# Reordering the first 50 microseconds of a fused attention and expert kernel: which work goes ahead of the first score step

## The reference

```python
def reference(x, w_attn, w_proj, decay_raw, W1, W2, Wr):      # x: 8 x 512 x 128
    xn = layernorm(x)                       # over the 128 channels
    # attention, 16 heads of 8 channels, causal
    q, k, v = split(xn @ w_attn)
    logw = -log1p(softplus(decay_raw)[h] * log1p(distance))
    y = softmax(q @ k.T / sqrt(8) + causal + logw) @ v
    attn = y @ w_proj
    # experts: 8 of them, the best 2 for each token
    probs = softmax(xn @ Wr.T); gate = top 2 of probs, normalised
    ffn = sum over the 2 experts of gate * (silu(xn @ W1[e].T) @ W2[e].T)
    return x + attn + ffn
```

## Time and profile before

| | us |
|---|---|
| median of 3 runs | 505.39 (504.28 to 505.66) |
| the profiled execution | 506.12 |
| its span, first to last instruction | 504.4 |
| what lies around the span | 1.72 |
| mean granted TensorE clock | 0.997 |
| PE busy over the span | 478.1 (95%) |
| DVE, POOL, ACT busy | 365.7, 366.2, 336.6 |

### The profile page before, as it was taken

The page is one execution under the profiler, slowest core; times in us unless marked ns, Lnnn a source line. Parts: engine busy times, 40 slices in busy tenths (PEclk is TensorE's granted clock), DMA queues, the critical chain, the costliest instruction groups (busy, mean ns, idle before and its releaser), DMA issues.

```text
span 504.4 us, 13425 instructions
## 1 busy us (share of the span) xinstructions
PE 478.1 (95%) x4294; PEld 346.7 (69%) x4294; DVE 365.7 (73%) x1407; ACT 336.6 (67%) x621; POOL 366.2 (73%) x591
## 2 busy tenths in 40 slices
PE   6769899999999999999999999989999999999997
PEld 5645465555664665566566556689999999999564
DVE  7888989988999989989889897733333333333887
ACT  4789878888888888887988888752233233232762
POOL 3587987889888889889889888734454554555784
PEclk9998999999999999999999999999999999999999
DMA  6479790780470461353255153877676777672634
GB/s 188 126 278 286 201 215 16 213 199 18 133 215 28 143 182 57 122 158 102 90 159 138 51 183 112 227 223 238 199 210 208 210 208 207 191 216 69 246 118 140
DMA packets 72755, 82.24 MB, mean 163 GB/s; under 512 B 8638, under 2 KB 52704, under 8 KB 72688
## 3 DMA queue, kind: packets, MB, share of 16 engines
q1 hardware_dynamic: 68368, 72.91, 50.3%
q0 software_dynamic: 4320, 8.47, 4.7%
HBM read 49.94 MB, written 31.86 MB: 162 GB/s over the span
## 4 chain that ended last, share of the span: by engine, by line
PE 69%; DVE 17%; ACT 10%; issue 2%; DMA 1%; SPq 0%; ACTq 0%; DVEq 0%
PE psT L1498 22%; PE psT L1585 13%; PE ps L1558 12%; PE psO L1518 11%; DVE scores L1268 8%; PE ps L1470 6%; ACT probs L1008 4%; ACT scores L965 3%; PE psM L1446 2%; DVE x_all L608 2%; PE ps L1549 1%; ACT values L992 1%; DVE xt L1122 1%; DMA w_qkv<-w_attn 1%; DVE probs L1054 1%
## 5 line engine op out<-in xcount | busy, mean ns | idle before, releaser
L1268 DVE CUSTOM_DVE_ANT_0 scores<-ps,wdist 128x256 f32<-128x256 f32 (+3 forms) x512 | 217.3, 485 | 22.6 <-PE ps L1470 21.8
L1008 ACT ACTIVATE probs<-psT 128x512 f32<-128x512 f32 x320 | 173.8, 597 | 50.3 <-PE psT L1498 49.1
L875 POOL TENSOR_SCALAR scores<-scores,row_max 128x256 f32<-128x256 f32 (+3 forms) x388 | 185.3, 493 | 29.2 <-DVE row_max L1268 28.1
L1498 PE MATMUL psT<-ident,scores 128*128 128x128 f32 x1280 | 176.3, 281 | 5.7 <-ACT probs L1008 5.6
L1498 PEld LDWEIGHTS psT<-ident,scores 128*128 128x128 f32 x1280 | 137.7, 141 | 64.0 <-issue 46.3
L894 POOL DMA_INDIRECT picked_dram<-scores,row_ring x71 | 69.8, 983 | 70.0 <-DVE scores L1349 66.8
L1017 ACT ACTIVATE scores<-ps 128x512 f32<-128x512 f32 x71 | 42.3, 598 | 91.4 <-PE ps L1558 91.4
L1518 PE MATMUL psO<-probs,values 128*32 128x512 f32 (+3 forms) x1024 | 88.4, 441 | 0.0
L965 ACT ACTIVATE scores<-scores,row_max 128x512 f32<-128x512 f32 x124 | 83.0, 727 | 0.0
L1585 PE MATMUL psT<-xn_all,scores 128*128 x568 | 75.4, 276 | 1.6 <-ACT scores L1017 1.6
L1558 PE MATMUL ps<-scores,wdist 128*128 128x128 f32 x568 | 74.9, 275 | 0.6 <-DMA wdist<-w1t 0.6
(11 more groups left out here) (169 smaller groups left out, 295.3 us busy)
## 6 DMA issues: line engine op xcount, KB each, us to landing
wdist<-w1t SPq DMA_DIRECT2D x71, 256.0 KB, 3.4
k_rows<-k_dram SPq DMA_DIRECT2D x64, 96.0 KB, 3.0
q_rows<-q_dram SPq DMA_DIRECT2D x64, 96.0 KB, 2.9
row_ring<-rows_dram SPq DMA_DIRECT2D x71, 65.0 KB, 2.9
rows_dram<-row_ring SPq DMA_DIRECT2D x6, 650.0 KB, 6.3
k_dram<-k_parts SPq DMA_DIRECT2D x7, 384.0 KB, 2.4
q_dram<-q_parts SPq DMA_DIRECT2D x7, 384.0 KB, 2.6
xn_all<-picked_dram SPq DMA_DIRECT2D x4, 512.0 KB, 7.4
```

Source lines behind the costliest of these rows:

```text
L875: last = nc.gpsimd.tensor_scalar(part, part, -1.0, row_max[:, r, tile, quad:quad + 1], ALU.mult, ALU.add)
L1008: nc.scalar.activation(probs[:, at.ring(2), w, :], psT[:, w % 2], ACT.Exp, scale=-1.0).then_inc(exp_ready, 1)
L1268: last = nc.vector.tensor_tensor_reduce(out=scores[:, r, u, col:col + n], in0=bank[:, col:col + n], in1=wdist[:, at.g * QUADS + quad, SEQ ...
L1498: last = nc.tensor.transpose(psT[:, w % 2, place * P:(place + 1) * P], scores[:, at.ring(2), u, col + key * P:col + (key + 1) * P], ident[:])
```

## The change

It alters the order of steps and the waits that go with it. No arithmetic is added or removed except warm-up matmuls.

1. The weights' DMA is issued ahead of the decay vector's.
2. `scaled_weights` leaves part 0 of BN and becomes a step of its own, WQ, behind NX. KA of batch 0 gets a wait for the centred weights.
3. The second warm-up stretch shrinks from 8 to 2.
4. In the prologue, BN part 1 is cut after 8 of its 12 tiles, and the last 4 with its sums and RS 1 go behind VL of batch 0. RT 0 goes from behind VL of batch 1 to behind VL of batch 3 and waits for that copy.
5. The turn of batch 6, VL of batch 4, and the turn of batch 7 (with LN 7) go ahead of the first score step; VL of batches 5, 6, 7 and LN 8 to 15 move up by one P1 step each in slot 0.
6. The last 4 tiles' statistics with the sums and RS of part 3 go into slot 1 (behind P1 steps 0 and 1). RT 1, RO 1 and LC go behind P1 step 4 of slot 1, CZ 2 behind step 3.
7. In slot 29, MI goes ahead of ACT's share of the maxima (SA). In slot 32, the second part of PV goes behind a TE step.

```diff
+EARLY = {0: {1: (("VL", 20), ("LN", 8), ("LN", 9)),
+             2: (("VL", 24), ("LN", 10), ("LN", 11), ("CZ", 1)),
+             3: (("VL", 28),) + tuple(("LN", h) for h in range(12, 16)) + (("TL", 0),),
+             4: (("XN", 4),) + ...
-         1: {2: tuple(("LC", b * GROUPS) for b in range(1, BATCH)) + (("CZ", 2),), 4: (("CZ", 3),)}}
+         1: {0: (("BN", 0, 3, 28, 32),), 1: (("RS", 3),), 3: (("CZ", 2),),
+             4: (("RT", 1), ("RO", 1)) + tuple(("LC", b * GROUPS) for b in range(1, BATCH)) + (("CZ", 3),)}}
...
-    step("PV", n - 2, NGROUP, 1)
+    if n != NGROUP:
+        step("PV", n - 2, NGROUP, 1)
...
+    if n == NGROUP:
+        step("PV", n - 2, NGROUP, 1)
     step("TE", n - 1, NGROUP, 4, 6)
...
+    if n == EXPERT_SLOT - 1:
+        steps.append(("MI", 0))
     if n >= GROUPS_BY_POOL:
         step("SA", n, NGROUP, (6, 7))
...
 PROLOGUE = [
-    ("BN", 0, 0, 0, 4), ("RS", 0), ("WU", 5), ("WC", 0), ("WU", 8), ("NX", 0), ("LN", 0), ("LN", 1), ("XB", 0), ("LN", 2),
-    ("KA", 0), ("QA", 0), ("BN", 0, 1, 4, 16), ("RS", 1), ("XB", 4),
+    ("BN", 0, 0, 0, 4), ("RS", 0), ("WU", 5), ("WC", 0), ("WU", 2), ("NX", 0), ("WQ", 0), ("LN", 0), ("LN", 1), ("XB", 0),
+    ("LN", 2), ("KA", 0), ("QA", 0), ("BN", 0, 1, 4, 12), ("XB", 4),
     ("KR", 0), ("QR", 0), ("KM", 0), ("QM", 0), ("KL", 0), ("QL", 0), ("LN", 3), ("CZ", 0),
     ("KW", 0, 0), ("QW", 0, 0), ("KD", 0), ("QD", 0),
-    ("XB", 8), ("VL", 0), ("BN", 0, 2, 16, 20), ("XB", 12), ("VL", 4), ("RT", 0), ("BN", 0, 2, 20, 24), ("RS", 2), ("LN", 4),
-    ("XB", 16), ("VL", 8), ("BN", 0, 3, 24, 32), ("RS", 3), ("LN", 5), ("XB", 20), ("VL", 12), ("LN", 6),
+    ("XB", 8), ("VL", 0), ("BN", 0, 1, 12, 16), ("RS", 1), ("XB", 12), ("VL", 4), ("BN", 0, 2, 16, 20), ("LN", 4),
+    ("XB", 16), ("VL", 8), ("BN", 0, 2, 20, 24), ("RS", 2), ("LN", 5), ("XB", 20), ("VL", 12), ("RT", 0), ("LN", 6),
+    ("BN", 0, 3, 24, 28), ("XB", 24), ("VL", 16), ("LN", 7), ("XB", 28),
     ("RO", 0), ("KW", 0, 1), ("QW", 0, 1), ("RB", 4), ("KD", 1), ("QD", 1), ("VS", 4), ("VS", 8), ("VS", 12)]
...
                 sp.dma_start(x_all[:, 0:TILES, :], x_rows(0)).then_inc(first_x_loaded, 16)
+                sp.dma_start(w_qkv[:], w_attn).then_inc(w_loaded, 16)
                 sp.dma_start(decay_in[:], decay_raw.rearrange("(a h) -> a h", a=1).broadcast_to([P, HEADS])
                              ).then_inc(decay_loaded, 16)
-                sp.dma_start(w_qkv[:], w_attn).then_inc(w_loaded, 16)
...
-                        scaled_weights()
                         dve.wait_ge(dve_init, 1)
...
-                run_prologue({**number_parts, "BN": norm_stats, "NX": normalise})
+                run_prologue({**number_parts, "BN": norm_stats, "WQ": scaled_weights, "NX": normalise})
...
-                    pe.wait_ge(vo_free, BATCH if n else 2)
+                    pe.wait_ge(vo_free, BATCH if n else 4)
...
-                    if b == 3:
+                    if b == 4:
                         pe.wait_ge(rstd_copied, 1)
-                    if b == 4:
                         pe.wait_ge(misc_free, MISC["KA", 0] + 1)
...
                         elif kind == "KA":
                             pe.wait_ge(xt_copied, 1)
+                            pe.wait_ge(centred_copied, 1)
```

More of the change, by code:

```diff
@@ L85 @@
 TOPK = 2
[L86 to L89, removed]
+EARLY = {0: {1: (("VL", 20), ("LN", 8), ("LN", 9)),
+             2: (("VL", 24), ("LN", 10), ("LN", 11), ("CZ", 1)),
+             3: (("VL", 28),) + tuple(("LN", h) for h in range(12, 16)) + (("TL", 0),),
+             4: (("XN", 4),) + tuple(
                  (kind, b * GROUPS) for kind, b in (("VS", 4), ("VS", 5), ("VS", 6), ("VS", 7), ("XS", 2), ("XS", 3), ("XS", 4),
                                                     ("XS", 5), ("XS", 6), ("XS", 7)))},
-         1: {2: tuple(("LC", b * GROUPS) for b in range(1, BATCH)) + (("CZ", 2),), 4: (("CZ", 3),)}}
+         1: {0: (("BN", 0, 3, 28, 32),), 1: (("RS", 3),), 3: (("CZ", 2),),
+             4: (("RT", 1), ("RO", 1)) + tuple(("LC", b * GROUPS) for b in range(1, BATCH)) + (("CZ", 3),)}}
 FIRST_ROWS_SLOT, ROW_TILES = 1, 4
@@ L246, in slot_steps @@
     steps.extend(("PA", 0, *part) for part in SUMS.get(n, ()))
-    if n == EXPERT_SLOT - 1:
-        steps.append(("MI", 0))
     if (n - 2) % PAIR == PAIR - 1:
@@ L1072, in norm_stats, with scaled_weights @@
                                                op0=ALU.max, op1=ALU.add).then_inc(decay_ready, 1)
-                def scaled_weights():
+                def scaled_weights(at):
                     dve.wait_ge(centred_full, 1)
```

## The result

The changed kernel takes 508.88 us (median of 10, 504.15 to 510.74) against 505.60 of before (median of 10, 503.04 to 506.87), a ratio of 1.0062 (95% interval 1.0033 to 1.0092): slower by 3.3 us, where 503.4 was forecast. The profiled execution took 504.15 us; the forecast of it was 504.07. It was the fastest of the ten and the only one with a granted clock of 1.000; the others had 0.986 to 0.993.

The account below looks back on a forecast made before the run. PE was taken to bound the middle (busy 95% of the span), so gains come only where it waits. Head start 1.65 plus 0.4 at R1 gave 2.05 us: 506.12 to 504.07, or 503.4 at the median; range 502.4 to 506.0.

Parts of the forecast that it names:

- Decay vector: Front, normalisation's chain: issued behind the weights, the vector delays it by 0.4 us, at worst 1.3.
- Clock: Front, PE: a low clock costs 0.2 us on the turn, half its price, and nothing on key and query products.
- the slower rival: Front: low clock lasts past the products through the next turns and first value product; 507.1 us, chance 0.11.
- Decay late: Front, rival: the decay vector lands with the weights, 0.9 us more on the normalisation; 504.3 us, chance 0.09.
- low clock: Front, two rivals: low clock through key and query products, 505.3 us, chance 0.20; or beyond them, 507.1, chance 0.11.
- nearest row: Phrase absent from the prediction given; on the clock it cites warm-up durations and 0.50 after a 2.40 us wait.
- 1.65: Front: the head start in us, 1.85 won at the turn less 0.2 for the clock.
- the 0.4 at R1: Slot 1, routing's first step R1: 0.4 us gained beyond the front's head start, bounds -0.5 and 1.6.
- WQ behind NX ... the new wait in KA is free: Front: two DVE copies cost 0.6 us, hidden by ACT's copy of the turned tokens; 0.3 without that cover.
- Slot 29 and the drain ... 0: Moving MI gains 0 us (bounds -0.3 and 0.2); moving a PV part in the drain 0 (to 0.1).
- Whatever this moment gains goes on to the end: From R1 on: the gain there persists, since what follows is work in fixed order with no fixed time.
- The scale: Whole kernel: the profiled run lies 0.73 us above the median 505.39, so 504.07 becomes 503.4 on the median's scale.

Follow-up runs that it names:

- e1: The changed kernel, unedited, run again: 511.18 us, ratio 1.0109; its profiled execution took 509.81 us.
- e17: The changed kernel with 12 more TensorE passes in slot 1, where it waits for the first exponentials: 508.34 us, ratio 1.0033.
- e3: The kernel before with only its second warm-up stretch cut from 8 to 2: 509.45 us, ratio 1.0060.
- e4: The kernel before with items 1 to 3 only (DMA order, WQ behind NX, 2 pairs of warm-ups): 509.05 us, ratio 1.0070.
- e15: The changed kernel, unedited, profiled once more: that execution took 507.54 us.
- e8: The kernel before with item 2 alone (WQ behind NX, and KA's wait): 505.61 us, ratio 0.9991.
- e6: The kernel before with items 4 to 7 alone: 505.95 us, ratio 1.0005.
- e5: The changed kernel with 8 pairs of warm-ups and the decay vector's DMA issued first again: 505.72 us, ratio 1.0002.
- e13: The changed kernel with six more pairs of warm-ups behind the turn of batch 0, ahead of the key product: 507.49 us, ratio 1.0024.
- e7: The changed kernel with 8 pairs of warm-ups, decay vector first, and 2 more pairs behind the first turn: 505.25 us, ratio 0.9985.

## Why the prediction was wrong, step by step

- **Decay vector: "I take 0.4 ... at worst it lands with the weights at 5.9 and costs 1.3 us".** This is the step that failed first, a term of the sum that was too small. In the eight profiles that have it behind the weights dec_neg came at 4.7, 5.3, 5.3, 5.5, 5.6, 5.8, 6.3 and 6.7: 0.1 to 2.1 later than the 4.60 of before, a median near 1. I had let one row, 2.8 us for a transfer that stood in front, speak for one that stands behind 196 KB. The bound was wrong too, in its reason: issued first, the weights land 2.8 to 3.0 us after 1.30, so at 4.1 to 4.3, not at 5.9 (nor only half a us earlier than before's 6.13), and in e1 the vector came 2.5 us after them, at 6.7. So "it lands with the weights" gives neither the time nor a bound. (The rule cited for it, "DMA: Bandwidth & Descriptors", Queues, rings and completion order, in the Trainium skill, agrees with the order in all eight: none came before the weights. It gives no price.) What it shares the engines with in those 2.5 us, the other tokens' DMA issued at 2.31 among it, wasn't tried.
- **Clock: "0.2 for the turn ... and nothing for the products".** This is the second step that failed, a term put at nothing. I had looked at the gap with a decay slip of 0.4, some 0.6 us. At 0.51 and 1.18 us it is indeed nothing (1.12 and 1.13 us for the key passes). At 1.43 to 3.11 it is 0.2 to 0.95 for the key passes, 0.7 to 0.9 for the query passes, and up to 0.9 for the next eight turns. The price per product (0.87) was about right (0.95 and 0.89 in e1). The point from which the slower rival decides, a low clock at VL of batch 0, was reached in e17 alone (1.56 us for its first eight passes); in e1, e3, e4 and e15 they took 1.09, as in after. It was named by the clock, not by what comes before it: PE's gap, that is the decay vector.
- **The rivals were kept apart.** "Decay late" stood at 504.3 with 0.09 and "low clock" at 505.3 and 507.1 with 0.20 and 0.11. They are one case: the late vector makes the gap that costs the clock, and item 3 took away the passes that would have covered it. The sum priced the 12 warm-ups at nothing but time. Together they give R1 at 46.5 to 48.5 and 507.5 to 509.8 us, outside the range. The slower rival had the right sign, 507.1, 1.8 us too little, and part of the mechanism: the low level does reach the next turns (1.55 us for eight in e1), but in no profile of the changed kernel the value product it counted in, and the late vector and the longer expert stretch, which do cost time, are not in it.
- **"nearest row" for the gap.** The before kernel has no gap there at all, so no row of it could show what a pause does ahead of the products. The row with a clock of 0.50 after the 2.40 us wait did show it elsewhere; I cited it and did not use it.
- **Where the vector was in time, the sum held, in part by luck.** XB 0 at 8.28 (8.75 forecast), first score step 22.02 (22.3), table load 31.06 (31.4), R1 43.81 (44.05) with DVE waiting 1.24 (1.6) for POOL's logits, the releaser I had named; own time 504.15 (504.07). Part of that is errors that cancel: the turn won 2.3 and not 1.65, and the 0.4 at R1 was not there (from turn to R1 35.5 us before and after; POOL ends last there where DVE did, at the same moment). The stretch of the experts took 0.6 more.
- **"WQ behind NX ... the new wait in KA is free"**: right (e8). **Items 4 to 7**: I gave them 0.4 at R1; e6 and e5 against e8 say 0. **"Slot 29 and the drain ... 0"**: no run told them from 0; they are in e6.
- **"Whatever this moment gains goes on to the end".** Half right: from R1 to the first expert turn it took 281.8 us before and 281.5 to 281.7 in the four profiles of after. The expert stretch, though, scatters by up to 3.6 us and was longer in nearly every profile with 2 pairs. That what follows is in a fixed order does not make its time fixed.
- **The scale.** I moved the sum from the profiled run to the median as if a kernel's executions lay as close as those three (504.28 to 505.66). The changed kernel's lie over 6.6 us, and in its four profiles it is the landing of one 8 KB transfer that goes with the clock its products get.

## What to carry to other kernels

Warm-ups that compute nothing cover a variable landing as well as hold the clock. Before shortening them, ask how late the last input of the next real matmul can be, not how late it was in one profile, and leave passes for that, but not without measure: 5 to 12 pairs took the same time here, 20 pairs 0.7% more. When an edit makes one engine wait for a transfer and another takes away what filled the wait, price the pair. If a profile agrees with a sum, compare its own time and its granted clock with the other runs before trusting it: here 504.15 us at 1.000 stood against a median of 508.88 at 0.991.

## What the runs showed of the hardware that I had not expected

- An 8 KB transfer issued behind one of 196 KB landed 2.8, 3.5, 3.5, 3.7, 3.7, 3.9, 4.4 and 4.9 us after its issue in eight profiles, and 2.7 to 3.3 in the twelve that have it first. The weights, in turn, landed 3.4 to 4.3 us after their issue as the second and 2.8 to 3.0 as the first.
- A pause of 1.18 us ahead of the turn left the key passes at 1.13 us and the query passes at 1.02. Key and query passes took 1.35 and 1.91 us behind a pause of 1.43, 2.07 and 1.71 behind 1.49 (e3), 1.36 and 1.91 behind 1.62, 2.08 and 1.91 behind 2.34 and 3.11. In e3 the four warm-ups ahead of the pause were at the high level already, in e4 and e15 (1.43 and 1.62) still at the low one. The length of the pause alone does not order the key passes.
- The clock that the profile prints does not show the low level at the start. From 6 to 8 it is 1.00 in the profile of after, where the four warm-ups take 421 ns each, and from 10 to 12 in e13, where ten passes do; at the high level such a pass takes 275. Durations tell the level there, and the mean of 1.000 is of the printed clock.
- A low stretch in slot 1 comes with such a front and without it: 0.50 from 30 to 34 in e13, 0.62 from 34 to 40 in e15, 0.64 from 30 to 34 in e17, but also 0.50 from 38 to 44 in e7, with 8 pairs. The kernel before has 0.50 from 38 to 39, and 0.78 over 34 to 40.
- Twenty pairs of warm-ups, all at the high level, cost 4.35 us at the median, of which R1 showed 0.9.
